# Experts chosen ahead of the norm: a routing rewrite in the second cross-attention of a two-layer decoder

## The reference

```
x5     = layernorm(x4 + cross_attention(x4, ctx))
logits = x5 @ gate_w.T
probs  = softmax(logits); the 8 largest choose the experts and weigh them
x6     = layernorm(x5 + sum over the 8 of prob * w2_e(silu(w1_e x5) * (w3_e x5)))
```

## Time and profile before

| what | value |
|---|---|
| median of 3 runs | 836.79 us (836.4 to 839.68) |
| profiled execution | 839.84 us, span of its instructions 838.2 us |
| busy, share of the span | PE 88%, DVE 59%, ACT 38%, POOL 36% |
| instructions of PE | 5,559 matmuls and as many weight loads |
| mean granted TensorE clock | 0.945 of full speed |
| HBM traffic | 166 GB/s over the span |

### The profile page before, as it was taken

The page is one execution under the profiler, slowest core; times in us unless marked ns, Lnnn a source line. Parts: engine busy times, 40 slices in busy tenths (PEclk is TensorE's granted clock), DMA queues, the critical chain, the costliest instruction groups (busy, mean ns, idle before and its releaser), DMA issues.

```text
span 838.2 us, 16078 instructions
## 1 busy us (share of the span) xinstructions
PE 738.2 (88%) x5559; PEld 602.5 (72%) x5559; DVE 492.6 (59%) x1484; ACT 314.5 (38%) x772; POOL 299.8 (36%) x395
## 2 busy tenths in 40 slices
PE   8999999989999999999977756554999888988986
PEld 6678888877878888888844433333998887887865
DVE  4877878755566666666788454331655445443335
ACT  3455555523434343444335322221332222244325
POOL 1211122221242121212210544456565455455545
PEclk9999999999999999999999786755999999999999
DMA  9454620000423243423035448114978888733357
GB/s 262 81 167 128 193 70 7 2 1 19 140 70 139 71 139 86 131 92 93 33 115 139 129 131 280 66 62 147 327 227 257 285 266 287 251 100 114 105 196 275
DMA packets 85300, 119.08 MB, mean 142 GB/s; under 512 B 28312, under 2 KB 59838, under 8 KB 84965
## 3 DMA queue, kind: packets, MB, share of 16 engines
q1 hardware_dynamic: 76052, 100.72, 39.1%
q0 software_dynamic: 9168, 17.35, 5.7%
HBM read 103.45 MB, written 35.58 MB: 166 GB/s over the span
## 4 chain that ended last, share of the span: by engine, by line
PE 40%; issue 14%; another core or an unknown queue 6%; DMA 5%; DVE 4%; SPq 3%; ACT 3%; POOL 2%; DVEq 0%; ACTq 0%; POOLq 0%
PE ps L190 37%; DMA rows_e<-x_slots 3%; PE ps L193 2%; ACT pTc L1535 1%; SPq L1894 1%; DVE topc L1590 1%; DMA rowso<-y_slots 1%; DMA y_slots<-o_e,index_e 1%; DMA out<-yo 1%; SPq L1902 0%; SPq L1378 0%; DVE h_e L2065 0%; ACT gate_e L2014 0%; DVE junk_e L2029 0%
## 5 line engine op out<-in xcount | busy, mean ns | idle before, releaser
L2084 POOL DMA_INDIRECT y_slots<-o_e,index_e x127 | 124.5, 980 | 102.8 <-DVE o_e L2075 58.3
L190 PE MATMUL ps<-xT_e,w_slot 128*128 128x128 f32 x760 | 98.7, 280 | 4.1 <-issue 3.0
L190 PEld LDWEIGHTS ps<-xT_e,w_slot 128*128 128x128 f32 x760 | 91.9, 196 | 6.6 <-issue 5.1
L2065 DVE TENSOR_TENSOR h_e<-ps,gate_e 128x256 f32<-128x256 f32 x64 | 27.0, 421 | 109.2 <-ACT gate_e L2014 71.7
L1688 POOL DMA_INDIRECT x_slots<-rows_all,index_all x64 | 62.3, 973 | 22.4 <-issue 17.6
L2008 ACT COPY xT_e<-ps 128x512 f32<-128x512 f32 x64 | 37.1, 580 | 76.9 <-PE ps L193 40.6
L190 PE MATMUL ps<-x_hi,w_hi 128*128 128x512 f32 x192 | 62.2, 405 | 1.6 <-POOL w_lo L1179 1.5
L1590 DVE TENSOR_REDUCE topc<-ps 128x4 f32<-128x1024 f32 x32 | 38.2, 1221 | 36.7 <-remote 30.1
L190 PE MATMUL ps<-x_lo,w_hi 128*128 128x512 f32 x192 | 59.6, 391 | 0.0
L190 PE MATMUL ps<-x_hi,w_lo 128*128 128x512 f32 x192 | 59.4, 390 | 0.0
L2014 ACT ACTIVATE gate_e<-ps 128x256 f32<-128x256 f32 x64 | 24.6, 384 | 87.8 <-remote 47.2
(11 more groups left out here) (302 smaller groups left out, 1695.1 us busy)
## 6 DMA issues: line engine op xcount, KB each, us to landing
w_slot<-in_we SPq DMA_DIRECT2D x95, 384.0 KB
rows_e<-x_slots SPq DMA_DIRECT2D x127, 136.0 KB
x_slots<-blank SPq DMA_DIRECT2D x4, 2176.0 KB, 9.7
sums<-key_sums SPq DMA_DIRECT2D x15, 512.0 KB, 4.2
w_kept<-in_we SPq DMA_DIRECT2D x20, 384.0 KB
wh<-in_wqkv SPq DMA_DIRECT2D x16, 384.0 KB, 5.3
rowso<-y_slots SPq DMA_DIRECT2D x10, 512.0 KB, 7.2
w_early<-in_we SPq DMA_DIRECT2D x12, 384.0 KB, 5.0
```

What stands on the lines that cost most here:

```text
L190: return self.pe.matmul(out, lhsT, rhs, start=start, stop=stop, skip_group_check=shared)
L2065: dve.tensor_tensor(T.h[:, 0:n, :].rearrange("p s t -> p (s t)"), ExpertBanks(m, p - 1).up[:, 2 * P:(2 + n) * P], T.gate[:, 0:n, :].rearra ...
L2084: pool.indirect_dma_start(m.y_slots, bass.IndirectOffsetOnAxis(ap=T.index[:, s:s + 1], axis=0), T.o[:, s, :], None, bounds_check=TOK * TOP ...
```

## The change

- The gate weights lose their mean over the 256 features (once, on PE and DVE). A norm subtracts a token's mean and multiplies by a positive number, so with such weights the logits of `x4 + attention` are those of x5 up to that number, and rank the same.
- x4 is transposed beside the maxima, in the same ring turn and step of PE, and copied by ACT. The step "back" now also makes the logits: x4T and `avT` times the gate, four matmuls into one sum. The steps x5T and gate are gone (10 steps instead of 12 on PE; the rank waits for `slot0` where it waited for `counted`).
- DVE copies the logits to SBUF and chooses on them at once; the sum, the variance, the slots and the norm's end come behind, in this order. The maximum that the exponentials subtract is the first of the eight times the root; the exponentials use the root as scale and nobody waits for them before the experts' weighing.
- POOL waits for `index` and `norm5`. All four orders are new, and the ring follows `CROSS_PE`.

```diff
-CROSS_POOL = ("pqr0s100002111132222433335444465555766677767")
+CROSS_PE = ("00100010202103012011312121432241232433432433554436546456455757565657667676677777")
+CROSS_ACT = ("0100000230111211412222230335433443441642755565553666645767777767")
+CROSS_DVE = ("pppqrs0000110qrsqr1122221033020331010144342422s142135335552663546634644637477574555576666677777")
+CROSS_POOL = ("pqr000s1200111122223343334544455556666767777")
...
# pe_cross1, sequence(b)
+            for k in range(KD):
+                last = tr(t.x4T_bank(b)[:, k * P:(k + 1) * P], m.x_all[:, b, k * P:(k + 1) * P])
             last.then_inc(*t.topT_ps.one)
...
         if b == 0:
+            pe.wait_ge(*t.gate_in(1))
+            for k in range(KD):
+                last = mm(t.gate_mean, m.mean128[:, :], r.gate[:, k, :], start=k == 0, stop=k == KD - 1)
+            last.then_inc(*t.gate_mean_ps.one)
...
-            last = tr(t.av_bank[:, u * P:(u + 1) * P], t.avT[:, u, :])
+            tr(t.result[:, u * P:(u + 1) * P], t.avT[:, u, :])
+        pe.wait_ge(*t.x4T(b + 1))
+        for part, turned in enumerate((L.x4T, t.avT)):
+            for k in range(KD):
+                last = mm(t.logits, turned[:, k, :], r.gate[:, k, :], start=part == k == 0, stop=part == k == 1, shared=True)
         last.then_inc(*t.back_ps.one)
-        yield
-        pe.wait_ge(*t.norm5(b + 1))
...
-            last = tr(t.x5T_bank[:, k * P:(k + 1) * P], r.rows[:, b, k * P:(k + 1) * P])
...
-            last = mm(t.logits, L.x5T[:, k, :], r.gate[:, k, :], start=k == 0, stop=k == KD - 1)
# dve_cross1, sequence(b)
         dve.wait_ge(*t.back_ps(b + 1))
+        if b >= LANES:
+            dve.wait_ge(*t.gexp(b - LANES + 1))
+        c = chain(dve.tensor_copy(L.scores[:, :], t.logits))
+        dve.wait_ge(*c)
+        c = chain(dve.max(L.best[:, :], L.scores[:, :]))
+        dve.wait_ge(*c)
+        c = chain(dve.match_replace(L.left[:, :], L.best[:, :], L.scores[:, :], LOWEST))
+        dve.wait_ge(*c)
+        dve.tensor_scalar(L.chosen[:, :], L.left[:, :], LOWEST / 2, None, ALU.is_lt).then_inc(*t.chosen.one)
+        yield
+        dve.tensor_tensor(L.res[:, :], t.result, m.x_all[:, b, :], ALU.add).then_inc(*t.added5.one)
...
+        yield
+        dve.wait_ge(*t.root5(b + 1))
+        dve_norm_end(m, r.rows[:, b, 0:D], L.res[:, :], L.mv).then_inc(*t.norm5.one)
+        dve.tensor_scalar(one[:, 0:1], L.best[:, 0:1], L.mv[:, 3:4], -1.0, ALU.mult, ALU.mult).then_inc(*t.gbias.one)
# pool_cross1
         pool.wait_ge(*t.index(b + 1))
+        pool.wait_ge(*t.norm5(b + 1))
```

More of the change, by code:

```diff
@@ L148, in weave, with bank_turns @@
         next(lanes[lane])
+def bank_turns():
+    at, turns = [0] * NSEQ, []
+    for b in map(int, CROSS_PE):
+        name = CROSS_STEPS[at[b]]
+        at[b] += 1
+        turns += [(b, name, j) for j in range({"scores": 2, "turned": 2, "tops": 1}.get(name.split()[0], 0))]
+    return turns
 def spread(ap, n, axis):
@@ L1277, in __init__ @@
         self.ps = m.ps
-        self.ring = [(b + ahead, name, j) for b in range(-1, NSEQ) for name, ahead in CROSS_TURNS if 0 <= b + ahead < NSEQ
-                     for j in range(1 if name == "tops" else 2)]
+        self.ring = bank_turns()
         self.av_bank = m.ps[:, 6, :]
         self.av = [m.ps[:, 6, e * D:(e + 1) * D] for e in range(2)]
-        self.x5T_bank = m.ps[:, 7, 0:D]
-        self.logits = self.rank = m.ps[:, 7, 0:NE]
+        self.result, self.logits, self.gate_mean = m.ps[:, 6, 0:D], m.ps[:, 6, D:D + NE], m.ps[:, 6, 0:NE]
+        self.rank = m.ps[:, 7, 0:NE]
     def bank(self, b, name, j):
@@ L1347, in __init__ @@
         self.top = s("top", [P, KD, 2 * P + HDX])
-        self.res, self.x5T = s("res", [P, D]), s("x5T", [P, KD, P])
-        self.left, self.slot = s("left", [P, NE]), s("slot", [P, NE])
+        self.res, self.x4T = s("res", [P, D]), s("x4T", [P, KD, P])
+        self.scores, self.left, self.slot = s("scores", [P, NE]), s("left", [P, NE]), s("slot", [P, NE])
         self.chosen, self.best = s("chosen", [P, NE], BF16), s("best", [P, TOPK])
@@ L1456, in values @@
                 pe.wait_ge(*t.vpair_in[n](i + 1))
-                if b:
+                if b == 0:
+                    pe.wait_ge(*t.gate_set(1))
+                else:
                     pe.wait_ge(*t.added5(b))
@@ L1509, in sequence @@
         if b:
-            pe.wait_ge(*t.counted(b))
+            pe.wait_ge(*t.slot0(b))
         mm(t.rank, m.before[:, :], L.chosen[:, :], stop=False)
@@ L1529, in sequence @@
         yield
+        act.wait_ge(*t.topT_ps(b + 1))
+        if b >= LANES:
+            act.wait_ge(*t.back_ps(b - LANES + 1))
+        act.copy(L.x4T[:, :, :].rearrange("p k t -> p (k t)"), t.x4T_bank(b)).then_inc(*t.x4T.one)
+        yield
         for e in range(2):
@@ L1542, in sequence @@
         yield
[L1543 to L1549, removed]
+        act.wait_ge(*t.gbias(b + 1))
+        act.activation(r.exp_all[:, b, :], L.scores[:, :], ACT.Exp, bias=L.one[:, 0:1], scale=L.mv[:, 3:4],
+                       accum_out=r.exp_sum[:, b:b + 1]).then_inc(*t.gexp.one)
         yield
@@ L1592, in sequence @@
                 yield
+        if b == 0:
+            dve.wait_ge(*t.gate_mean_ps(1))
+            for k in range(KD):
+                last = dve.scalar_tensor_tensor(out=r.gate[:, k, :], in0=t.gate_mean, scalar=-1.0 / KD, in1=r.gate[:, k, :], op0=ALU.mult, op1=ALU.add)
+            last.then_inc(*t.gate_set.one)
         dve.wait_ge(*t.topT_ps(b + 1))
@@ L1606, in sequence @@
         dve.wait_ge(*t.back_ps(b + 1))
-        dve.tensor_tensor(L.res[:, :], t.av_bank[:, 0:D], m.x_all[:, b, :], ALU.add).then_inc(*t.added5.one)
+        if b >= LANES:
+            dve.wait_ge(*t.gexp(b - LANES + 1))
[8 more added lines that the diff above has]
+        dve.tensor_tensor(L.res[:, :], t.result, m.x_all[:, b, :], ALU.add).then_inc(*t.added5.one)
         dve.wait_ge(*t.added5(b + 1))
         dve_norm_begin(m, L.res[:, :], L.stats[:, :], L.mv).then_inc(*t.var5.one)
[L1610 to L1619, removed]
-        c = chain(dve.match_replace(L.left[:, :], L.best[:, :], exps, -1.0))
-        dve.wait_ge(*c)
-        dve.tensor_scalar(L.chosen[:, :], L.left[:, :], 0.0, None, ALU.is_lt).then_inc(*t.chosen.one)
         yield
@@ L2033, in weigh @@
         b, k = divmod(n, TOPK)
+        if n == 0:
+            dve.wait_ge(*tc.gexp(NSEQ))
         if n >= TOPK:
```

43 lines of the change are left out of this document (17 added, 26 removed).

## The result

Twenty runs of each kernel: before 839.13 us (median), after 843.22, ratio 1.0044 with a 95% interval of 1.0026 to 1.0062. By the ratio the change makes the kernel slower by some 3.7 us; 5.3 us faster was forecast. The time lies inside the stated range of 821 to 845, but in the part of it that was there for the rivals. The rival "longer runs hold PE longer" had priced 841.6, +4.8 over its base.

What follows compares the result with a forecast made beforehand. No engine was saturated in cross1 after the first scatter; PE's held signals, then POOL's scatters at its end, set the time. Terms -4.7 - 1.0 + 0.4 = -5.3 took the median 836.79 to 831.5 us, range 821 to 845.

Steps and rivals of the forecast that it cites:

- longer runs hold PE longer: Rival for cross1's end: joined scatters of 4 and 5 delay PE's signals and 6; +4.8, 841.6 us; chance 0.27.
- the gap goes: End of cross1: 5's rows ready while 4's are sent, POOL then bounds; 7's first scatter at 566.0, -4.7 us.
- 7's own path: End of cross1: 7 ready 5.1 us after its back ends at 557.44, so 562.5, before POOL reaches it at 566.0.
- The start of cross1: Before the first scatter: +0.4 us for gate-mean work; first scatter within 3 us of 460.82, taken as 0.
- 4's scatters start 1.0 earlier: Middle of cross1: 4's norm's end becomes DVE's next step; -1.0 us taken, between bounds of -3.1 and +3.
- much faster: Rival in cross1: fewer PE signals make holds cheaper; -33 us at most, half gives 820; chance 0.08.
- Passed on in full: Experts' stage: it is PE's and moves as a block, so the whole -5.3 us reaches the kernel's time.
- no change: Rival: a hold outlasts 4's scatters by 5 us, or the early part loses the gain; 836.5 us; chance 0.23.
- the slower case: The outcome over 841.0 us, from longer scatter runs holding PE: rival's chance 0.27, 0.05 within the band, 0.24 stated.
- The port: Scatters beside DVE's work: by the skill's rule eight norm's ends could each hold one, sum -3.0; forecast kept 1.27 us a scatter.
- the costs that the forecast called hidden: Cross1: extra DVE work, +0.15 us a sequence, and PE gate passes, 1.4 us a sequence, covered by idle time.

Runs made afterwards that it cites:

- experiment 4: Kernel after, with POOL waiting between 4's last scatter and 5's first for the signal of 6's columns: 838.85 us, ratio 1.0007 to before.
- experiment 6: Kernel before with POOL waits for the next transposed sum amid scatters: of 4 only, 835.4 us (0.9938); of 0 to 4, 826.48 us (0.9848).
- e10_orders: Kernel after, first norm's end straight behind the first slots on DVE, POOL's roots of 2 and 6 and 7's scatters moved: 836.45 us, 0.9935 of before.
- experiment 7: Kernel after with other DVE and POOL orders, 836.45 us; with three added POOL waits 836.81; with four waits on held PE signals instead 829.97 (0.9877).
- e2_seven_first: Kernel after, with POOL issuing 7's first six scatters ahead of 6's last two: 842.68 us, ratio 1.0033 to before.
- Experiment 3: Kernel after in arithmetic and steps, with the kernel before's orders less the dropped steps and x4T's copy placed earlier on ACT: 870.78 us, ratio 1.0326.
- e7_pause: The run of experiment 4: kernel after with a POOL wait for 6's columns ahead of 5's scatters, 838.85 us, ratio 1.0007.
- experiment 5: 64 small matmuls ahead of either kernel to move PE's refills: 781.74 us before and 798.22 after without holds, 842.09 after with holds.
- e4_phase: Kernel after with 64 small matmuls added to the warm-up, on the chip without holds: 798.22 us, ratio 1.0208 to before.
- b1_phase: Kernel before with 64 small matmuls added to the warm-up, on the chip without holds: 781.74 us, ratio 0.9998.
- e8_three: Kernel after with pause before 5's scatters, 7's first six ahead of 6's last two, first norm's end behind first slots; chip without holds: 798.23 us, 1.021.
- b3_pause: Kernel before with a POOL wait amid 4's scatters for 5's transposed sum, on the chip without holds: 782.12 us, ratio 1.0009.
- b3b_pause: Kernel before with a POOL wait amid 4's scatters for the transposed sum of 5, on a chip with holds: 835.4 us, ratio 0.9938.

## Why the prediction was wrong

**The step that failed** is "the gap goes. Late next is POOL ... hence 566.0 instead of 570.72: -4.7". The gap went, but it was also a place where PE's signals came out. With 4's and 5's scatters joined, 6's columns came 5.8 us late and 6's logits were held to 2.5 us behind the run's end (558.35 against 555.87); what was late next was 6, not POOL. From 4's first scatter to 7's first the forecast had 31.9 us instead of 36.6 (the -4.7); measured are 40.4 (574.15 - 533.75), +3.8 for the term. Putting a gap of 2 us back (experiment 4) returned some 3 us, stopping POOL in four runs of the kernel before returned 13 us (experiment 6), and waits added to `e10_orders` 5 us by the ratios (experiment 7). That holds pace this stretch, and that closing the gap costs time by them, is shown. It is not the whole miss: the forecast was off by 9 us, and with the gap back the kernel is still no faster than before.

**The rival** had the mechanism and nearly the size: 6 ready at 565, measured 562.65; 7's first at 575.5, measured 574.15; +4.8, measured +3.7. It did not have the place, so the close number is in part luck: it let 6's values wait for the run's end, but ACT copied them at 542.60, no later than before; 6's columns and logits were late instead. It had 0.27 against 0.42 because one run of before, from 552.26, held nothing. What spares that run stays open; the steps of PE there are short and few.

**7's own path.** The forecast had 7 ready at 562.5; the profile after has its norm's end at 571.57 + 0.41. The length was right: from the end of back's transposes to the norm's end 5.1 us were forecast, and 571.98 - 566.83 = 5.2 measured. The start was wrong: the division into `avT` ran at 565.66, where before back itself was issued at 557.00, because 7's turned scores were held too. So 7, ready at 572.0, also missed the forecast's 566.0, and `e2_seven_first` shows POOL waiting for it.

**The start of cross1** was taken as 0, "within 3 us"; it is +7.0. DVE's rows, 0's index and 0's norm's end:

```profile
464.10 0.17 DVE L1645 TENSOR_SCALAR index_all<-rows_all 128x8 uint32<-128x8 f32 x1
465.52 0.23 DVE L1625 COPY scoresc<-ps 128x64 f32<-128x64 f32 x1 [1.24 <-PE ps L201]
...
466.47 0.41 DVE L222 TENSOR_SCALAR rows_all<-resc,mvc 128x256 f32<-128x256 f32 x1
```

The index is there 3.8 us later than before (464.27 against 460.51), and the norm's end stands behind the choice of 1, another 2.6 us. Experiment 3 had the old order of DVE and started no sooner, so the order of the maxima alone is not it. 4's first scatter is no later for it: from the first scatter to 4's first it is 65.9 us instead of 73.3. So "4's scatters start 1.0 earlier" came out at -0.4 as a sum of two terms, +7.0 and -7.4, that the forecast did not have. The second looks like the gain of fewer hand-overs that "much faster" had named; no run separates it, and none moves the first scatter alone where there are holds, so what the late start costs there stays open.

**Passed on in full** was right: +3.4 at SP's first load, +3.7 by the ratio.

**Slips in the sums**, none of which moves the forecast: "no change" adds 10.6 to 559 and gets 569.6, hence 835.7 and not 836.5; -5.3 + 8 x 0.28 is -3.1; and by the shares given, the slower case keeps 0.22, not 0.24.

**The port.** By the rule of the Trainium skill's page "SBUF — State Buffer", Who interferes with whom, packed scatters could each be held by DVE. The line's own view has almost the figures of the earlier trace rows:

```profile
L1706 POOL DMA_INDIRECT x_slots<-rows_all,index_all x64: 954/960/1242, 467.8 to 583.0; - x64
```

But that view is of little weight, since only two of the eight norm's ends of the kernel after fell beside a scatter (538.52 and 571.57), both started inside one, and both scatters took 1.04 us like those with none beside. The other order stands in the kernel before: the norm's end starts 0.16 us ahead of the scatter of 562.93, and that one takes 1.17 us.

```profile
562.77 0.41 DVE L211 TENSOR_SCALAR rows_all<-resc,mvc 128x256 f32<-128x256 f32 x1 [1.83 <-issue]
```

The same pair stands in `e7_pause` (566.11 and 566.27, 1.16 us). So the rule may be at work here, at 0.13 us a time and seldom more than once or twice a profile, not at 8 x 0.28. The Trainium skill's page "Runtime: NRT & Kernel Launch", Instruction fetch mechanics, calls refills mostly hidden: experiment 5 agrees, with and without holds.

**On the chip without holds** the two variants of the kernel after lost 2.1%, 16 us. There POOL hardly stops before the change. In `e4_phase` 7's first scatter is 19.1 us later than in `b1_phase` (552.45 against 533.39), and its rows split that: the first scatter 8.9 (468.83 against 459.92), more idle time and roots of POOL 7.6, two more scatters ahead of it 2.5. Behind the first scatter the longest idle time is for the root of 2, with four of 0's scatters ready:

```profile
478.90 0.65 POOL L218 TENSOR_TENSOR mvc<-mvc,power 128x1 f32<-128x1 f32 x1 [3.77 <-DVE mvc L214]
```

The root of 6 behind 5's scatters makes DVE wait for 6.97 us there (540.37) but stops POOL for 1.2 only. `e8_three` lost as much with a first scatter only 3.3 us late (462.85 against 459.60 in `b3_pause`), so a late start is not the whole of it. The unchanged kernel after never ran there; that it too loses is argued from these rows, not shown. What the costs that the forecast called hidden would show there, no run separates.

## What to carry to other kernels

A gap on one engine may be the moment in which another's signals get through: before closing it, look at who resumes right behind each run, and count their waits for a "remote" releaser as part of what the gap does. If a burst of indirect DMAs holds others up, a short wait in its middle for the signal that is held can pay more than it costs (1.8 us of waiting bought 5.2 in `b3b_pause`); it must be put on a signal that isn't out yet, which only the profile of the very same orders shows. Time a kernel on more than one chip before its orders are tuned to waits like these.

## What the runs showed of the hardware

- On two of the three chips PE's completion signals come late while POOL issues indirect DMAs back to back. Some are out within the run (columns ended at 543.90, taken at 549.73, 5.8 us late; the run ends at 555.87). The rest come out behind the run's end, 1.5 us in the kernel before (544.01, taken at 545.49), 2.4 us in the kernel after (555.87, taken at 558.24); pauses of 2.0 and 1.8 us were enough. Without scatters none was over 0.5 us late. This was so in four of the five groups, and in the traces of the result.
- The chip of the second group shows none of it, with the same scatters at the same 1.27 us: 781.85 us instead of 839, SP's first expert load at 534.4 instead of 573.2 (profile of `b3_pause`), and 244 us from there to the end instead of 265. The experts' stage has holds too: in the whole profile of before ACT's gates wait 47.2 us for "remote". It was one group on one chip, so whether it is the chip or a state that it was in is not shown.
- What starts a hold is open. It isn't a refill of PE's program within the run, and not scatters alone. Whether the number of scatters or their bytes matter, and whether it is POOL's issuing or the traffic of the DMAs, was not tried.
